# Reporting a landing before the next scatter is issued, and sharing the last step between GpSimd and VectorE

## The reference

```python
xn = _layernorm(x, axis=-1)
s = _L1_attn_ref(xn, ...)              # a scan over the rows, 128 -> 128
# per row: softmax over 8 experts, the best 2 kept and normalised
h   = gelu(einsum('bsd,edf->ebsf', xn, W1) + b1)       # 128 -> 512 for each expert
y_e = einsum('ebsf,efd->ebsd', h, W2) + b2             # 512 -> 128
y   = einsum('ebsd,bse->bsd', y_e, P_norm)             # two experts count for each row
x = x + s * silu(y)
```

## Time and profile before

| what | value |
|---|---|
| median of three runs | 464.46 us |
| the profiled execution, whole | 466.61 us |
| its span, first to last instruction | 464.9 us |
| TensorE busy | 418.2 us, 90% |
| VectorE busy | 284.0 us, 61% |
| ScalarE busy | 215.4 us, 46% |
| GpSimd busy | 155.8 us, 34% |
| granted TensorE clock, mean | 0.974 |

### The profile page before, as it was taken

How to read it: one execution, slowest core, us unless ns; L and a number is a source line. 1 busy time by engine, 2 the same in 40 slices (tenths; PEclk the granted TensorE clock), 3 DMA queues, 4 the chain that set the end, 5 groups by cost and what they waited for, 6 DMA issues and landing times. The chain is left out here.

```text
span 464.9 us, 9785 instructions
## 1 busy us (share of the span) xinstructions
PE 418.2 (90%) x2912; PEld 352.1 (76%) x2912; DVE 284.0 (61%) x1137; ACT 215.4 (46%) x525; POOL 155.8 (34%) x215
## 2 busy tenths in 40 slices
PE   6989988999999999998987989489799999999873
PEld 5967666878878889687776879388689899998631
DVE  2688889887887889888757476103133344343327
ACT  3274546555544746524425343214256555555512
POOL 6420014024034231533242014513344455555410
PEclk9999999999999999999999989779899999999998
DMA  7379011363172231121223213411122222222577
GB/s 187 105 147 168 8 37 35 75 196 87 33 199 75 83 75 38 42 77 43 63 55 91 50 32 91 117 45 45 47 61 66 70 69 75 68 70 70 147 253 216
DMA packets 63426, 40.80 MB, mean 88 GB/s; under 512 B 18324, under 2 KB 56088, under 8 KB 63384
## 3 DMA queue, kind: packets, MB, share of 16 engines
q1 hardware_dynamic: 58688, 31.27, 27.2%
q0 software_dynamic: 4352, 8.99, 5.8%
q10 hardware_dynamic: 344, 0.03, 0.1%
HBM read 21.78 MB, written 18.48 MB: 87 GB/s over the span
## 5 line engine op out<-in xcount | busy, mean ns | idle before, releaser
L690 POOL DMA_INDIRECT routed<-send,slot x64 | 65.0, 1015 | 128.3 <-DMA routed<-send,slot 50.6
L699 POOL DMA_INDIRECT results<-nat,y_to x72 | 70.1, 974 | 107.0 <-DVE nat L1634 85.1
L1025 PE MATMUL psA<-xuT,w_all 128*128 128x256 f32 x288 | 71.3, 391 | 3.7 <-ACT h1T L1235 3.2
L1235 ACT ACTIVATE h1T<-psA,b1T 128x256 f32<-128x256 f32 x144 | 62.8, 475 | 15.8 <-PE psB L1048 12.7
L1025 PEld LDWEIGHTS psA<-xuT,w_all 128*128 128x128 f32 x288 | 52.0, 195 | 12.5 <-ACT h1T L1235 3.6
L1606 DVE TENSOR_SCALAR xu<-ring 128x256 f32 (+1 forms) x38 | 11.3, 298 | 80.4 <-DMA ring<-routed 56.0
L1037 PE MATMUL psC<-w_all,h1T 128*128 128x128 f32 x464 | 57.1, 276 | 0.9 <-DVE nat L1618 0.9
L1037 PEld LDWEIGHTS psC<-w_all,h1T 128*128 128x128 f32 x464 | 54.5, 193 | 1.5 <-ACT h1T L1235 1.1
L1226 ACT ACTIVATE xuT<-psB 128x256 f32<-128x256 f32 x37 | 14.2, 384 | 63.4 <-PE psB L1015 38.2
L839 PE MATMUL psB<-xnT,w_l 128*128 128x512 f32 x64 | 34.2, 615 | 0.5 <-ACT selT L1155 0.5
L851 PE MATMUL psB<-w_l,hg0T 128*128 128x128 f32 x256 | 32.9, 281 | 0.0
(11 more groups left out here) (289 smaller groups left out, 865.0 us busy)
## 6 DMA issues: line engine op xcount, KB each, us to landing
ring<-routed SPq DMA_DIRECT2D x38, 130.0 KB
inv<-inv_room SPq DMA_DIRECT2D x8, 512.0 KB
w_all<-results SPq DMA_DIRECT2D x15, 256.0 KB, 4.5
routed<-ring SPq DMA_DIRECT2D x24, 130.0 KB, 6.1
n_room<-nT SPq DMA_DIRECT2D x8, 256.0 KB
w_all<-in_L_ffn_W_dram SPq DMA_DIRECT2D x1, 2048.0 KB
out_dram<-x_all SPq DMA_DIRECT2D x8, 256.0 KB, 2.3
results<-nat,y_to POOLq DMA_INDIRECT x72
```

The lines of the kernel that those rows point to most:

```text
L690: pool.indirect_dma_start(routed[:, :], bass.IndirectOffsetOnAxis(ap=slot[par][:, c, t:t + 1], axis=0), send[par][:, c, t, :], None).then_ ...
L699: pool.indirect_dma_start(results[:, :], bass.IndirectOffsetOnAxis(ap=y_to[:, par, a:a + 1], axis=0), yw[:, par, a, :], None).then_inc(S[f ...
L1025: last = mm(psA[:, j // 2, (j % 2) * UNIT:(j % 2 + 1) * UNIT], w1_all[:, e, j * P:(j + 1) * P], xuT[:, :], start=True, stop=True)
L1235: f(h1T[:, j, :], psA[:, j // 2, (j % 2) * UNIT:(j % 2 + 1) * UNIT], ACT.Gelu, bias=b1T[:, n:n + 1]).then_inc(S["gelu_ready"], 1)
```

## The change

There are two edits. In `send_results`, the wait for the landing of unit u - 1 and the raise of `y_landed` stand ahead of the wait for `yw_ready` and the two indirect DMAs of unit u; they stood behind them. At the end, groups 1 and 4 are finished by GpSimd after it has raised `all_landed`. ScalarE writes the silu of these two into the buffers `th0` and `mix`, which are free by then, and GpSimd multiplies there in place and adds to `x_all`. VectorE keeps the other six. SyncE stores in the order 0, 2, 1, 3, 5, 6, 4, 7.

```diff
+    POOL_ENDS = (1, 4)
+    DVE_ENDS = tuple(g for g in range(groups) if g not in POOL_ENDS)
+    END_ORDER = (0, 2, 1, 3, 5, 6, 4, 7)
...
+        end_pool = [th0, mix]
...
-            for g in range(groups):
-                sp.wait_ge(S["x2_ready"], g + 1)
+            for g in END_ORDER:
+                if g in POOL_ENDS:
+                    wait_on(sp, "x2_pool", POOL_ENDS.index(g) + 1)
+                else:
+                    wait_on(sp, "x2_ready", DVE_ENDS.index(g) + 1)
                 sp.dma_start(out_rows[:, g * TILES:(g + 1) * TILES, :],
                              x_all[:, g * TILES:(g + 1) * TILES, :]).then_inc(S["x_out"], 16)
...
             def send_results(u, par):
 
+                if not (isinstance(u, int) and u == 0):
+
+                    pool.wait_ge(S[f"y_sent{1 - par}"], (u + par) * (8 * HALVES))
+                    pool.sem_inc(S["y_landed"], 1)
                 wait_on(pool, "yw_ready", u + 1)
                 pool.sem_inc(apart, 1)
                 for a in range(HALVES):
                     pool.indirect_dma_start(
                         results[:, :], bass.IndirectOffsetOnAxis(ap=y_to[:, par, a:a + 1], axis=0),
                         yw[:, par, a, :], None).then_inc(S[f"y_sent{par}"], 16)
-                if not (isinstance(u, int) and u == 0):
-
-                    pool.wait_ge(S[f"y_sent{1 - par}"], (u + par) * (8 * HALVES))
-                    pool.sem_inc(S["y_landed"], 1)
...
             pool.sem_inc(all_landed, 1)
+
+            for n, g in enumerate(POOL_ENDS):
+                ts = slice(g * TILES, (g + 1) * TILES)
+                m = end_pool[n][:, :, :]
+                wait_on(pool, "silu1_pool", n + 1)
+                pool.tensor_tensor(m, s1[:, ts, :], m, ALU.mult).then_inc(S["mix_pool"], 1)
+                wait_on(pool, "mix_pool", n + 1)
+                pool.tensor_tensor(x_all[:, ts, :], x_all[:, ts, :], m, ALU.add).then_inc(S["x2_pool"], 1)
...
             for g in range(groups):
                 act.wait_ge(S["sum_ps"], g + 1)
-                if g >= 2:
-                    act.wait_ge(S["mix_ready"], g - 1)
-                f(th1[g % 2][:, :, :], tiles(sum_ps_of(g)), ACT.Silu).then_inc(S["silu1_ready"], 1)
+                if g in POOL_ENDS:
+                    f(end_pool[POOL_ENDS.index(g)][:, :, :], tiles(sum_ps_of(g)), ACT.Silu
+                      ).then_inc(S["silu1_pool"], 1)
+                else:
+                    n = DVE_ENDS.index(g)
+                    if n >= 2:
+                        act.wait_ge(S["mix_ready"], n - 1)
+                    f(th1[n % 2][:, :, :], tiles(sum_ps_of(g)), ACT.Silu).then_inc(S["silu1_ready"], 1)
...
-            def finish(g):
+            def finish(n, g):
                 ts = slice(g * TILES, (g + 1) * TILES)
-                m = mix2[g % 2][:, :, :]
-                dve.wait_ge(S["silu1_ready"], g + 1)
-                v.tensor_tensor(m, s1[:, ts, :], th1[g % 2][:, :, :], ALU.mult).then_inc(S["mix_ready"], 1)
-                dve.wait_ge(S["mix_ready"], g + 1)
+                m = mix2[n % 2][:, :, :]
+                dve.wait_ge(S["silu1_ready"], n + 1)
+                v.tensor_tensor(m, s1[:, ts, :], th1[n % 2][:, :, :], ALU.mult).then_inc(S["mix_ready"], 1)
+                dve.wait_ge(S["mix_ready"], n + 1)
                 v.tensor_tensor(x_all[:, ts, :], x_all[:, ts, :], m, ALU.add).then_inc(S["x2_ready"], 1)
 
             dve.wait_ge(S["s1_ready"], groups)
-            for g in range(groups):
-                finish(g)
+            for n, g in enumerate(DVE_ENDS):
+                finish(n, g)
```

More of the change, by code:

```diff
@@ L385, in two_block_kernel @@
             "sum_ps", "mix_ready", "silu1_ready", "x2_ready", "x_out",
+            "silu1_pool", "mix_pool", "x2_pool",
         )}
```

## The result

The changed kernel takes 490.39 us (median of 4 runs, 486.44 to 492.38); the kernel before, run beside it, took 464.63 us. The ratio is 1.0555, with a 95% interval from 1.0488 to 1.0622: 5.6% slower. The profiled execution took 492.38 us with a span of 490.6 us, against 466.61 and 464.9 us before: 25.7 us more in the span.

What follows compares the result with a forecast made beforehand. TensorE was taken to set the units' 3.80 us pitch, VectorE the end. Terms 15.0 - 0.4 + 3.9 + 1.5 = +20.0 us gave 486.6 us from the profiled execution, 484.5 us from the median; range 471 to 493 us.

Steps and rivals of the forecast that it cites:

- as summed: Whole kernel: the slower GpSimd loop, a late landing and the end add up, 477 to 489 us; chance 65%.
- longer one: Rival: landings over 2.27 us, two in the loads, or GpSimd's products after VectorE's; 489 to 497 us; chance 15%.
- The loop: Stage of the units: GpSimd waits for each landing, pitch 4.4 us against TensorE's 3.80 us, +15.0 us over 25 pitches.
- From unit 34 to 35: Last pitch of the units: GpSimd's 4.4 us in place of today's 4.78 us, 0.4 us back.
- One landing in the loads: Last units: unit 35 or 34 issued behind a landing slowed beside the loads of results, +3.9 us.
- The end: Last stage: GpSimd finishes two groups, but its products and VectorE's operations exclude each other on SBUF, +1.5 us.
- GpSimd's lag: Stage of the units: GpSimd falls behind by nearly a pitch unnoticed, then VectorE and TensorE go at its pitch.
- the early report: VectorE's waits for the report: gain of at most 2.8 us without GpSimd's own pitch, none with it.
- The shorter loop: Rival, units: scatter preparation overlaps the landing wait, pitch 3.97 us, 469 to 473 us in all; chance 12%.
- faster: Rival: GpSimd's loop hides below 3.80 us and the end gains 2.66 us, 461.8 down to 459.0 us; chance 5%.

Runs made afterwards that it cites:

- e2_report_only: Kernel before with only the landing wait and report moved ahead of the issue, VectorE finishing all eight groups: 488.59 us, ratio 1.0535.
- e3_report_two_back: As e2_report_only, but the wait ahead of the issue asks for unit u - 2, and both counts are waited for at the end: 464.41 us, ratio 0.9991.
- e7_wait_between: Changed kernel with the landing wait and the raise between the wait for `yw_ready` and the two scatters: 480.14 us in one execution.
- e6_loads_last: Changed kernel with SyncE's first eight loads of results moved behind the last landing: 495.24 us in one execution.
- e4_end_in_psum: e1_end_only with silu of VectorE's six groups written back to PSUM and multiplied there in place: 462.41 us, ratio 0.9991 to the kernel before.
- e1_end_only: Changed kernel with the landing wait and report behind the issue again, only the shared end kept: 467.32 us, ratio 1.0075 to the kernel before.
- e5_both_mended: Edits of e3_report_two_back and e4_end_in_psum together: 461.28 us, ratio 0.9971 to the kernel before.
- e8_groups_2_5: e5_both_mended with GpSimd finishing groups 2 and 5 in place of 1 and 4, stores reordered: 461.33 us, ratio 0.9970 to the kernel before.

## Why the prediction was right

484.5 us was predicted, 490.39 us measured, inside the range of 471 to 493 us. The case "as summed" had 477 to 489 us; what came is 1.4 us above it, in the range of the "longer one", which had a chance of 15%. The mechanism was the one of the sum, the loop through one landing per unit. But the loop and the end were both put too low, and the late landing too high: between the profiled executions the terms give +20.0 us and the measurement +25.8 us.

- **The loop, +15.0 us for 25 pitches.** Right in kind, shown by e2_report_only against the kernel before and against e3_report_two_back, and by e7_wait_between. Its parts were 1.27 + 2.27 + 0.79 + 0.08 = 4.41 us; measured are 1.26 + 2.25 + 0.94 = 4.45 us. The step from the landing to the scatter was 0.07 us too short. Without the late landing the 25 pitches cost 23.0 - 3.1 = 19.9 us, 4.9 us more than the term. About 1.3 us of it are 25 times the 0.05 us. Most of the rest are single rounds that were longer: unit 25's first scatter came 7.1 us after unit 24's, with one landing of 3.89 us (412.78 us in the chain of waits) and a second scatter issued 2.25 us after the first, some 1 us late. Delays of both kinds are in the other runs too, the kernel before included, where unit 24's second scatter comes 2.25 us after its first and unit 13's landing takes 4.2 us, and nobody waits for them. What makes them is open. Where each round hangs on the one before it, such a delay is paid in full. I had put the whole term at a steady round.
- **From unit 34 to 35, -0.4 us.** Measured 465.42 - 460.99 = 4.43 us against 4.78 us: right.
- **One landing in the loads, +3.9 us.** It was unit 33's, 5.39 us, 3.1 us over 2.25; e6_loads_last showed its cause. The kernel before has two late ones there, unit 33's with 4.6 us and unit 34's; with the loop, unit 34 is issued only after unit 33 has landed, and then takes 2.24 us itself.
- **The end, +1.5 us.** Measured +3.1 us from the last landing to VectorE's end and +3.6 us to the span's end. This is the term that was furthest off for its size. GpSimd's product was put at 1.22 us by doubling a copy and took 1.26 us and more. The exclusion is real. Two things were not in the sum: VectorE idle for group 2, since GpSimd has taken the group that ScalarE delivers second (1.93 us, of which 1.34 us are left at the full clock in e4_end_in_psum), and the first sums at half the clock. On the other side only three of VectorE's operations were held, 2.8 us, where I had counted four, 4.3 us. To VectorE's end, the shared end alone costs 2.0 us, though with the clock at 0.73 and 0.60 in its first sums (e1_end_only), the report alone 1.6 us through the clock (e2_report_only).
- **GpSimd's lag.** That VectorE would be held by the report in most units was right: 21 times, 22.7 us. That the early report gives nothing was put on the loop. No run shows what it would give without the loop, as e3_report_two_back reports no earlier than the kernel before.
- **The rivals.** The shorter loop of 3.97 us rested on rows with no second wait between the landing and the scatter. e7_wait_between has just one wait there, too, and needs 4.27 us: from its second scatter to the next are 3.00 us, not the 2.70 us of the earlier trace rows. The trace's record of semaphore updates says why. In the earlier trace rows the last update for the landing comes at 293.01 us and the scatter starts 0.27 us later; the trace shows the wait as the scatter's own, with no instruction between. In 23 of the 24 places of the kernel before where this scatter (L690) waits so, the way is 0.27 us. In e7_wait_between the landing is recorded at 379.81 us, and the scatter starts 0.77 us later, behind the wait and the report, which are an instruction of their own. So the rival's reason holds for a wait in the scatter itself and not for these. By an estimate from these rows, a loop with such a wait would take 1.26 + 2.25 + 0.27 = 3.78 us, just under the 3.80 us that "faster" asked for. No run tried it, and no run came near 3.80 us with the loop.

Left open: why TensorE's clock was also low during the first sums of e1_end_only (0.73, after only 2.12 us of idle time), and in those of e5_both_mended (0.81, then 0.59, after 1.95 us), and 1.00 in e4_end_in_psum, which idled for 2.37 us there. How much of the difference ahead of unit 9 between e7_wait_between and the changed kernel is the kernel's is open, too.

## What to carry to other kernels

A wait that costs nothing behind an issue may cost a whole round trip ahead of it: add up issue, landing and the way from the wait to the next issue, and compare the sum with the pitch of the stage. If it is longer, ask for an older transfer, as the kernel before and e3_report_two_back do in the same place. Write down the order of one engine's queue before calling a moved wait earlier or later: two places in the source can be one place in the queue. Before a second engine is given a share of a chain, look whether the two read SBUF at once, which of the shares arrives first, and what closes that engine's program behind its last piece. Work in PSUM kept VectorE free of GpSimd here; then fuller transfers and GpSimd's DRAIN took back most of the gain.

## What the runs showed of the hardware

- From a wait that is an instruction of its own to the start of the indirect DMA behind it GpSimd needs 0.74 to 0.76 us; where the DMA itself waits for a landing, it starts 0.27 us after the landing's last update (23 of 24 places of L690 in the kernel before). Two such DMAs in a row start 1.27 us apart and leave 0.30 us between them. One more wait in the loop costs some 0.15 us of pitch (4.43 and 4.45 us against 4.27 and 4.30 us).
- A GpSimd product or sum of two 128x512 f32 tensors takes 1.26 to 1.27 us while VectorE reads one SBUF input at a time, and up to 1.77 us while it reads two.
- GpSimd's closing DRAIN ends 5.3 us after it starts behind a DMA's wait (446.87 us, kernel before), and 5.3 us after the end of a last addition (456.64 to 461.96 us, e8_groups_2_5).
- The landing of a pair of scatters, counted from the second one's start, takes 2.2 to 2.3 us in most units, and 4.6 to 5.4 us for unit 33 beside the loads in the changed kernel, e2_report_only and e7_wait_between.
